# Softmax scaled after the mix: turned reciprocals in the 3rd and 4th attention of a chain, and exponentials by head in the 4th

## The reference, cut to what matters

```python
# 3rd                                            # 4th
scores = q @ k.T / sqrt(16)                      attn = q @ k.T * 16 ** -0.5
scores = where(mask == 0, -1e9, scores)          attn = where(xa_mask, -finfo.max, attn)
e = exp(scores - max(scores)) * mask             attn = softmax(attn)
probs = e / (sum(e) + 1e-9)
out = (probs @ v) @ Wo.T + bo                    out = (attn @ v) @ proj_w + proj_b
```

## Time and profile before

| | before |
|---|---|
| median of 3 runs (lowest to highest) | 1398.53 us (1394.56 to 1402.86) |
| profiled execution, span of its instructions | 1401.9 us, 1400.1 us |
| busy: TensorE, VectorE, ScalarE, GpSimd | 1278.1, 1047.8, 677.4, 654.1 us |
| granted clock of TensorE, mean | 0.98 |

### The profile page before, as it was taken

How to read it: one execution, slowest core, us unless ns; L and a number is a source line. 1 busy time by engine, 2 the same in 40 slices (tenths; PEclk the granted TensorE clock), 3 DMA queues, 4 the chain that set the end, 5 groups by cost and what they waited for, 6 DMA issues and landing times.

```text
span 1400.1 us, 24568 instructions
## 1 busy us (share of the span) xinstructions
PE 1278.1 (91%) x9411; PEld 1026.3 (73%) x9411; DVE 1047.8 (75%) x2236; ACT 677.4 (48%) x1503; POOL 654.1 (47%) x760
## 2 busy tenths in 40 slices
PE   7599999959879999999999999999998999999987
PEld 5588887846667777777777787767776777777766
DVE  3478784547877888888888866888888788888863
ACT  4267766403344455545444553445544544455543
POOL 4354442012654554565555532464555555556462
PEclk9799999989999999999999999999999999999999
DMA  5523222010000000000000020000000000000000
GB/s 131 117 69 99 69 80 68 1 40 0 1 1 12 12 1 1 16 25 23 1 1 1 1 62 15 11 12 9 5 1 5 27 12 5 9 1 5 5 5 16
DMA packets 48469, 34.19 MB, mean 24 GB/s; under 512 B 22177, under 2 KB 45536, under 8 KB 48352
## 3 DMA queue, kind: packets, MB, share of 16 engines
q1 hardware_dynamic: 48304, 32.59, 8.7%
q10 hardware_dynamic: 48, 0.01, 0.0%
HBM read 23.26 MB, written 8.39 MB: 23 GB/s over the span
## 4 chain that ended last, share of the span: by engine, by line
PE 49%; DVE 33%; POOL 7%; SPq 4%; issue 3%; ACT 3%; DMA 1%; ACTq 0%; DVEq 0%
PE ps L876 6%; DVE mx L1379 6%; PE ps L904 5%; PE ps L925 5%; DVE mx L1390 5%; PE ps L817 4%; PE ps L851 4%; PE ps L861 4%; DVE zt L1357 3%; PE ps L972 3%; PE ps L911 3%; SPq L623 3%; DVE pr L1410 3%; PE ps L800 3%; DVE front L1410 3%
## 5 line engine op out<-in xcount | busy, mean ns | idle before, releaser
L1603 POOL TENSOR_TENSOR rstd<-mv,halfneg 128x1 f32<-128x1 f32 x192 | 109.6, 574 | 267.6 <-DVE mv L1348 266.8
L851 PE MATMUL ps<-wk,tt 128*128 128x308 f32 x512 | 148.0, 430 | 14.3 <-DVE pr L1385 14.2
L1432 DVE TENSOR_TENSOR xt<-xt,ps 128x256 f32<-128x256 f32 x160 | 66.1, 415 | 87.7 <-PE ps L925 52.1
L851 PEld LDWEIGHTS ps<-wk,tt 128*128 128x128 f32 x512 | 94.0, 192 | 48.1 <-DVE pr L1385 15.2
L1189 ACT ACTIVATE pr<-pr 128x616 f32<-128x616 f32 x128 | 90.3, 714 | 80.4 <-DVE pr L1385 44.7
L1193 ACT ACTIVATE front<-ps 128x512 f32<-128x512 f32 x96 | 57.0, 597 | 148.4 <-PE ps L876 148.4
L961 PEld LDWEIGHTS ps<-tt,fc 128*128 128x128 f32 x1024 | 117.7, 192 | 13.0 <-ACT tt L1165 9.5
L961 PE MATMUL ps<-tt,fc 128*128 128x128 f32 x1024 | 123.6, 278 | 0.9 <-ACT tt L1165 0.9
L1165 ACT ACTIVATE tt<-ps,cols 128x128 f32<-128x128 f32 x192 | 77.2, 454 | 87.2 <-PE ps L800 86.6
L1642 POOL TENSOR_TENSOR front<-mx,front 128x616 f32<-128x616 f32 x64 | 78.5, 1226 | 87.6 <-DVE mx L1379 87.4
L1357 DVE TENSOR_SCALAR zt<-xt,mv,rstd 128x256 f32<-128x256 f32 (+1 forms) x160 | 92.6, 579 | 31.7 <-POOL rstd L1603 30.6
(11 more groups left out here) (219 smaller groups left out, 3087.2 us busy)
## 6 DMA issues: line engine op xcount, KB each, us to landing
out_dram<-xt SPq DMA_DIRECT2D x64, 128.0 KB, 1.8
xt<-in_x_dram SPq DMA_DIRECT2D x32, 128.0 KB, 2.7
xt<-out_dram SPq DMA_DIRECT2D x32, 128.0 KB, 2.2
fc<-in_L_xattn_fc_w_dram SPq DMA_DIRECT2D x2, 1024.0 KB, 5.6
wk<-in_L_xattn_wkv_dram SPq DMA_DIRECT2D x4, 512.0 KB, 4.9
front<-in_L_xattn_wkv_dram SPq DMA_DIRECT2D x4, 512.0 KB, 4.3
wo<-in_L_xattn_wo_dram SPq DMA_DIRECT2D x1, 1024.0 KB, 6.7
kb<-in_L_xattn_wq_dram SPq DMA_DIRECT2D x1, 1024.0 KB, 8.4
```

The lines of the kernel that those rows point to most:

```text
L851: last = mm(bank(lane, k)[:, SFROM[k]:SFROM[k] + HB * KEYS], t[:, lane, kc, :], wk[:, kc, b, h0:h0 + HB * KEYS], start=kc == 0, stop=kc == ...
L1603: p.tensor_tensor(rstd[:, n:n + 1], mv[:, n, 1:2], halfneg[:, :], ALU.pow).then_inc(done["rstd"], 1)
```

## The change

The scores stay as they were, and the mix runs on probabilities that are not divided by their sum. `recip` runs once per attention and writes 256 reciprocals into `z`: the 16 sums, each repeated over the 16 columns of its head. A new step `rturn` turns them on TensorE (two transposes of 128x128 into bank 1), `rec_t` copies them to `z` on ScalarE, and `heads` on VectorE multiplies the turned mix with them into `t`. `weigh` (3rd) and `scale` (4th) are gone, and so is `mixed`. In the 3rd attention `pturn` waits for `maskmul`, and the two copies after it wait for the row sum, which reads the same buffer; `den_eps` runs once, on 16 columns.

In the 4th the query is scaled by -1/4 when it is copied, so that scores are negated; the mask adds instead of subtracting; `rowmax` takes the minimum; `below` and `rowsum` are gone. `expo` is eight activations of 77 columns, each with the least score of its head as bias and the sum accumulated into `rec`.

All five strings of `TURNS` are new, those of the first phase included, where the steps are the same.

```diff
-    top = ["scores", "rowmax", "shift"] if a is L1 else ["scores", "bound", "rowmax", "below"]
+    top = ["scores", "rowmax", "shift"] if a is L1 else ["scores", "bound", "rowmax"] + ["below"] * (a is L2)
-    norm = ["rowsum"] + ["den_eps"] * (a is L2) + ["recip", "weigh" if a in WEIGHED else "scale"]
+    norm = {L1: ["rowsum", "recip", "weigh"], L2: ["rowsum"], L3: []}[a]
...
-    steps += [(s, second) for s in masked + norm + turns] + [("mix", a.name)]
-    return steps + ([] if a is L1 else [("mixed", a.name), ("proj", a.name)]) + [("resid", a.name)]
+    steps += [(s, second) for s in masked + norm + turns]
+    if a is L1:
+        return steps + [("mix", "1"), ("resid", "1")]
+    return steps + [("den_eps", a.name)] * (a is L2) + [(s, a.name) for s in ("recip", "rturn", "rec_t", "mix", "heads", "proj", "resid")]
...
             def pturn(key, run):
-                s = "expo" if a is L0 else "weigh" if a in WEIGHED else "scale"
+                s = {"1": "weigh", "2": "maskmul"}.get(key[0], "expo")
...
+            def rturn(key, run):
+                lane = run.lane
+                pe.wait_ge(done["recip"], at("recip", key, run))
+                pe.wait_ge(done["pturn_rest"], at("pturn_rest", key + ".1", run))
+                for g in range(ATTN[key].groups):
+                    last = turn_in(bank(lane, 1)[:, g * P:(g + 1) * P], z[:, lane, g * P:(g + 1) * P], ident[:, :])
+                last.then_inc(done["rturn"], 1)
...
             def expo(key, run):
+                if key[0] == "3":
+                    for h in range(HG):
+                        own = v[:, h * KEYS:(h + 1) * KEYS]
+                        last = ac(own, own, ACT.Exp, bias=mx[:, lane, g, h:h + 1], scale=-1.0, accum_out=rec[:, lane, g, h:h + 1])
...
             def pturn_main(key, run):
                 act.wait_ge(done["pturn"], at("pturn", key, run))
+                if key[0] == "2":
+                    act.wait_ge(done["rowsum"], at("rowsum", key, run))
...
-            def mixed(key, run):
-                act.wait_ge(done["mix"], at("mix", key, run))
-                ac(t[:, run.lane, :, :].rearrange("p c n -> p (c n)"), bank(run.lane, 0)[:, 0:H], ACT.Copy).then_inc(done["mixed"], 1)
+            def rec_t(key, run):
+                act.wait_ge(done["rturn"], at("rturn", key, run))
+                ac(z[:, run.lane, 0:H], bank(run.lane, 1)[:, 0:H], ACT.Copy).then_inc(done["rec_t"], 1)
...
             def recip(key, run):
+                s, k = {"0": ("mix", key), "1": ("rowsum", key), "2": ("den_eps", "2"), "3": ("expo", "3.1")}[key[0]]
+                dve.wait_ge(done[s], at(s, k, run))
...
+                    dst = z[:, lane, 0:H].rearrange("p (h d) -> p h d", d=L2.hd)
+                    src = (rec if key == "3" else mx)[:, lane, :, :].rearrange("p g h -> p (g h)").unsqueeze(2).to_broadcast([P, 2 * HG, L2.hd])
+                v.reciprocal(dst, src).then_inc(done["recip"], 1)
...
             def heads(key, run):
+                    dve.wait_ge(done["mix"], at("mix", key, run))
+                    dve.wait_ge(done["rec_t"], at("rec_t", key, run))
+                    last = v.tensor_tensor(t[:, lane, :, :].rearrange("p c n -> p (c n)"), bank(lane, 0)[:, 0:H], z[:, lane, 0:H], ALU.mult)
```

More of the change, by code:

```diff
@@ L188 @@
 MADE_BY = {
-    "tensor": ("item_mm", "turn", "query", "scores", "pturn", "mix", "proj", "uproj", "ssm", "fc1", "fc2",
+    "tensor": ("item_mm", "turn", "query", "scores", "pturn", "rturn", "mix", "proj", "uproj", "ssm", "fc1", "fc2",
                "w2_mm", "wqt_mm", "k_mm", "wk_mm", "vt_mm", "vwo_mm", "v_mm", "scan_mm", "gap_turn", "more_pe"),
-    "scalar": ("item_act", "turned", "query_bias", "expo", "pturn_main", "mixed", "u_sb", "gelu", "w2_sb", "wqt_sb", "k1_sb", "vt_sb", "silu", "more_act"),
+    "scalar": ("item_act", "turned", "query_bias", "expo", "pturn_main", "rec_t", "u_sb", "gelu", "w2_sb", "wqt_sb", "k1_sb", "vt_sb", "silu", "more_act"),
     "vector": ("ctx_stats", "ctx_norm", "item_dve", "stats", "aggr", "norm", "bound", "rowmax", "shift", "rowsum", "den_eps", "recip", "weigh",
                "pturn_rest", "heads", "resid", "resume", "wk_sb", "vwo_sb", "k_sb", "v_sb", "carry", "ends", "gap", "agree"),
-    "gpsimd": ("ctx_rstd", "head_masks", "row_masks", "value_zero", "zeros", "rstd", "prebias", "keep", "below", "maskmul", "scale", "gain", "offset", "masks", "fold", "vtw_zero"),
+    "gpsimd": ("ctx_rstd", "head_masks", "row_masks", "value_zero", "zeros", "rstd", "prebias", "keep", "below", "maskmul", "gain", "offset", "masks", "fold", "vtw_zero"),
     "sync": ("load", "put", "get", "store", "weights_get", "wkv1_get", "v0_put", "v_lay")}
@@ L284 @@
     "sync": (
[L285 to L286 removed]
+        "a22aa3a1aaaaaaaa03a10aaaaaaa21003a321aa00a32112aa001312200aa33110a2aa230311322aaa3aa0011223a3300aaa22b10211303aa"
+        "0312021b0111332223300123b0001b11b2233b30212021133022130130021323"),
 }
@@ L921, in proj @@
                 else:
-                    pe.wait_ge(done["mixed"], at("mixed", key, run))
+                    pe.wait_ge(done["heads"], at("heads", key, run))
                 for kc in range(KC):
@@ L1102, in more_pe @@
                             mm(scan_out(l), ident[:, :], chunk_view(U[:, :, 1:S + 1])[:, :, :, l], start=False, stop=True).then_inc(more_mm, 1)
-            steps = {"item_mm": item_mm, "turn": turn, "query": query, "scores": scores, "pturn": pturn, "mix": mix, "proj": proj,
+            steps = {"item_mm": item_mm, "turn": turn, "query": query, "scores": scores, "pturn": pturn, "rturn": rturn, "mix": mix, "proj": proj,
                      "uproj": uproj, "ssm": ssm, "fc1": do_fc1, "fc2": do_fc2, "w2_mm": w2_mm, "wqt_mm": wqt_mm, "wk_mm": wk_mm, "k_mm": k_mm, "v_mm": v_mm,
@@ L1177, in query_bias @@
                 if key == "3":
-                    last = ac(q[:, lane, 0:H], bank(lane, 0)[:, 0:H], ACT.Copy)
+                    last = ac(q[:, lane, 0:H], bank(lane, 0)[:, 0:H], ACT.Copy, scale=-L3.scale)
                 else:
@@ L1284, in more_act @@
                     act.sem_inc(more_r, MORE)
-            steps = {"item_act": item_act, "turned": turned, "query_bias": query_bias, "expo": expo, "pturn_main": pturn_main, "mixed": mixed, "u_sb": u_sb,
+            steps = {"item_act": item_act, "turned": turned, "query_bias": query_bias, "expo": expo, "pturn_main": pturn_main, "rec_t": rec_t, "u_sb": u_sb,
                      "gelu": gelu, "w2_sb": w2_sb, "wqt_sb": wqt_sb, "k1_sb": k1_sb, "vt_sb": vt_sb, "silu": silu, "more_act": more_act}
@@ L1371, in bound @@
                     off = out3[:, run.batch, run.tile:run.tile + 1, :].to_broadcast([P, HG, KEYS])
-                    last = v.scalar_tensor_tensor(heads_view(key, run.lane), off, NEG, score_view(run.lane), ALU.mult, ALU.add)
+                    last = v.scalar_tensor_tensor(heads_view(key, run.lane), off, -NEG, score_view(run.lane), ALU.mult, ALU.add)
                 last.then_inc(done["bound"], 1)
@@ L1378, in rowmax @@
                 src = heads_view(key, run.lane) if s == "bound" else score_view(run.lane)
-                v.tensor_reduce(mx[:, run.lane, group(key), :], src, AX.X, ALU.max).then_inc(done["rowmax"], 1)
+                v.tensor_reduce(mx[:, run.lane, group(key), :], src, AX.X, ALU.min if key[0] == "3" else ALU.max).then_inc(done["rowmax"], 1)
             def shift(key, run):
@@ L1395, in den_eps @@
             def den_eps(key, run):
-                dve.wait_ge(done["rowsum"], at("rowsum", key, run))
-                m = mx[:, run.lane, group(key), :]
+                dve.wait_ge(done["rowsum"], at("rowsum", key + ".1", run))
+                m = mx[:, run.lane, :, :]
                 v.tensor_scalar(m, m, 1e-9, None, ALU.add).then_inc(done["den_eps"], 1)
```

140 lines of the change are left out of this document (69 added, 71 removed).

## The result

| | before | changed |
|---|---|---|
| median of 6 runs (lowest to highest) | 1398.44 us (1394.56 to 1402.86) | 1385.91 us (1383.59 to 1387.92) |
| profiled execution, span | 1401.9, 1400.1 us | 1383.7, 1382.0 us |
| first state-space matmul, from the span's start | 292.7 us | 273.1 us |
| from there to the end | 1107.4 us | 1108.9 us |

The ratio is 0.9909, 95% interval 0.9885 to 0.9933. The forecast, 1380 with a range of 1335 to 1425, holds the time. Its reason does not hold. The last two lines of the table split the span at the first matmul of the second phase, and all the gain stands ahead of it, in the first phase (here everything up to that matmul), whose steps the change leaves alone and only reorders. The changed attention comes out even in this pair of profiles; the experiments make it about 5 us slower.

What follows compares the result with a forecast made beforehand. It took no engine alone as the limit, the second phase's chain going between VectorE and TensorE. Terms -101 + 14 + 47 + 6 + 20 - 6 = -20 us took 1401.9, less 3.4, to 1378.5, said as 1380; range 1335 to 1425.

Steps and rivals of the forecast that it cites:

- The first 310 us unchanged within 2 us: First phase: same steps in a slightly other order, taken as unchanged within 2 us.
- First-phase times that moved: First phase: moved times there were listed among the signs that would show the prediction wrong; no size given.
- The sum of -20 us for the attention: Third and fourth attention: removed and added work with contention, priced by engine, were to total -20 us.
- Wide reciprocal, +47: VectorE, both attentions: 64 reciprocals of 128x256 at 1.4 us, 90 us at a price of 0.52, adding 47 us.
- Turning, +6: TensorE: two transposes x 64 at 0.11 us, 14 us at a price of 0.40, adding 6 us.
- ScalarE, +20: 4th attention: eight 77-column exponentials for one of 616, 185 us more busy, 11 us at 0.06, charged double as +20.
- Heads, +14: VectorE: scaling the mixed output, 64 multiplications of 128x256 at 0.42 us, 27 us busy, adding 14 us.
- Removed, -101: VectorE's weighing, row sums, small reciprocals and epsilons, and GpSimd's subtraction and scaling, taken out: -101 us together.
- Contention, -6: VectorE's first-attention weighings and norms: some 12 us of surplus go as GpSimd works less, -6 after the price.
- ScalarE did not become the wait: Rival: probability copies queue behind 4th-attention exponentials and TensorE waits, +67 instead of +20, 1425 us; chance 0.16.
- nothing: Rival: time taken from VectorE goes to TensorE's path or an ill-fitting order, 1392 to 1405 us; chance 0.16.
- dear reciprocal: Rival: wide reciprocal takes 2.1 to 2.8 us, its term 70 to 93 us, 1401 to 1425 us; chance 0.13.

Runs made afterwards that it cites:

- e6: Kernel before with GpSimd's masks step later and SP's load of lane 1's second tile of x earlier: 1385.32 us, ratio 0.9910.
- e1: Changed kernel with the order of the kernel before for all first-phase steps: 1406.63 us, ratio 1.0040 to the kernel before.
- e2: Kernel before, attention untouched, with the changed kernel's order for the first-phase steps alone: 1382.47 us, ratio 0.9871.
- e4: Changed kernel with each 128x256 reciprocal replaced by one of 128x16 and a copy that repeats it: 1337.85 us, ratio 0.9546.
- e9: Changed kernel without the turning of the reciprocals (128 transposes, 64 ScalarE copies); heads multiplies by the unturned tile: 1369.37 us, ratio 0.9803.
- e7: Changed kernel with one 128x616 exponential a group in the 4th attention for eight of 128x77, no least-score shift or sums: 1371.17 us.
- e8: Changed kernel without the sums that the 4th attention's exponentials accumulate; the reciprocals read another tile: 1372.76 us, ratio 0.9818.
- e10: Kernel before with the changed first-phase order, without the 3rd attention's 64 VectorE multiplications by the reciprocals: 1363.07 us, ratio 0.9762 to the kernel before.
- e12: Kernel before with the changed first-phase order, without GpSimd's subtraction and scaling passes over the 4th attention's scores: 1366.84 us, ratio 0.9790.

## Why the prediction was right in number and wrong in its reason

*The first 310 us unchanged within 2 us.* This is the step that failed, and it made the number: that 1386 lies near 1380 is luck. The prediction saw that all strings were new and did not look at what the old order lost: the stall at 46 to 55 us was to be seen in the trace, with both waits. The first phase gave 16 to 20 us, where the sum had nothing; two of its steps, the masks and one tile's load, gave 12 of them (e6). "First-phase times that moved" was one of the prediction's own signs of being wrong, and it is the one that came.

*The sum of -20 us for the attention.* Measured +1.5 in the first pair of profiles and about +5 in e1 and e2. By terms:

- *Wide reciprocal, +47.* The duration, 1.4 us, was too short: 1.745 measured. The prediction's other estimate, 2.3 us, worked out from the Trainium skill's "VectorE: DVE Perf Modes", section "Walkthrough: the 8-slice pipeline in each mode", was too long; the trace agrees with that rule in kind, a price per element, and not in size. The price, 0.52 a us, was too low: 0.7 by e4. At 0.7, 111.7 us are some 78 us, an estimate from e4's rate, 31 over the term. The place matters: the reciprocal follows the last copy in its tile, and TensorE and the heads wait for what it makes (e4, e9). The prediction's median of 2.5 to 4 us of cover at `rturn` was too hopeful: 40 of 64 were waited for, 49 us.
- *Turning, +6.* 15 measured (e9).
- *ScalarE, +20.* 13 to 15 measured (e7, e8), by a smaller busy time, 127 us and not 185, at about the doubled price that was charged (15/127 = 0.12 against 20/185 = 0.11); the sums have nearly all of it.
- *Heads, +14.* 416 ns each, as said; its price was not measured.
- *Removed, -101.* Three terms, together -83, gave -30 one at a time. Prices read as an engine's share of the chain say what lies on the path that ended last; they do not say how close the next path is. Take one step away and the path shifts, as e10's chain shows (VectorE 35% to 19%, TensorE 45% to 65%).
- *Contention, -6.* Of the right kind, and at least as large as said: e12 takes 23.5 us off VectorE's busy time by GpSimd's passes alone, where the term had 12 us of work. The norm of 128x256 fell from 601 to 500 ns in the changed kernel, but it stands at 590 ns in e12 as in e2, so that fall is not shown to be GpSimd's. (The 17 us of the weighings, which are the 2nd attention's, are 12 by the earlier trace rows, 32 x (233 + 150) ns; the term would be -5.)

VectorE's busy time came out at the 1013 us that was said because errors nearly cancel: the reciprocals took 22 us more than their 90, while the norms (13 us) and the epsilons (5 us more off than said) took less.

The terms measured one by one do not add up: +78, +15 and +15 added and -30 removed would make +78, and +5 was measured. Either the removed steps give more together than one by one, or the added ones cost less together (e4 and e9 both take away the same waits at the new transposes), or the new order of the second phase gave something, or the small reciprocals and the epsilons that no run took out. Which, stays open: no run took the removed steps out together, and these runs keep the order written for the steps that were still there.

*The rivals.* ScalarE did not become the wait (8% of the chain, 13 to 15 us). For the attention by itself, in the old first phase (e1: 0.4% over the kernel before, so some 1404 us), "nothing" (1392 to 1405) and "dear reciprocal" (1401 to 1425) both hold the time. The second names a cause that the runs show: its term of 70 to 93 us holds the 78, though by a higher price and not by the 2.1 us or more that it asked for. Neither had the first phase, or that the removed steps were worth a third of their price one at a time.

## What to carry to other kernels

Where a change also rewrites an order, split the span at the last step that the change leaves alone and compare the halves before any other reading; and look in the trace of before for stretches where all engines stand, since a new order may mend them by chance. When two waits end together, taking either away shows next to nothing: try both. Do iterated operations such as the reciprocal on the few values there are and copy the result wide; take the price of a step from where it stands in its tile, not from its engine's mean share of the chain.

## What the runs showed of the hardware

- VectorE's reciprocal costs by the element: 200 ns for 128x8, 246 for 128x16, 1745 for 128x256, so (1745 - 246)/240 = 6.2 ns an element, against the 1.0 ns that the prediction worked out from a reduction of 616 columns and a multiplication of 256. A copy that repeats 16 columns to 256 takes 384 ns.
- An exponential with an accumulated sum shows a second record of 188 ns. It lengthens a block of eight by 0.74 us (2.84 against 2.10), 93 ns a sum.
- Some of VectorE's instructions take longer beside GpSimd's: without GpSimd's two passes (162 us) the same VectorE instructions took 23.5 us less in all (e12 against e2). A weighing on `front` took 840 ns instead of 1034; the one on `pr` (1084) and the 128x256 norm (590) stayed.
